# Column maxima of an attention chunk: one VectorE reduction over two PSUM banks in place of two reductions over one

## The chip, the cores and the metric

The kernel runs on one core of a Trainium2 chip. The metric is the device time of one execution in microseconds (us). The times of the kernel before are three runs; one further execution was profiled, and all rows shown come from it.

## The reference

Eight images of 64 channels and 56 x 56 pixels go through a group norm and a 3x3 convolution with a residual, then, with the 3136 pixels of an image as tokens of 64 channels, through self attention within the image, and through a mixture of 16 experts of which each token takes two. Cut to what matters here:

```python
x = x + conv3x3(group_norm(x), weight)
t = to_tokens(x)                                   # 8 x 3136 x 64
n = layer_norm(t)
q, k, v = n @ Wq.T + bq, n @ Wk.T + bk, n @ Wv.T + bv
attn = softmax(q @ k.T / 8, axis=-1)               # 3136 x 3136 per image
t = t + attn @ v
t = t + top2_of_16_experts(layer_norm(t))
```

The softmax needs, for each query, a bound on its scores to be subtracted in the exponent. The kernel computes the maximum of the query's scores over all 3136 keys.

## The kernel before

An image is cut into 7 chunks of 448 tokens (`CHUNK`), a chunk into 4 tiles of 112. There are 56 chunks over the 8 images, and the program is written out in full, with one body for each chunk and some bodies before the first and after the last. A body has 25 steps, `i` from 0 to 24, one for each block of 128 keys (`KEY_TILES`). Each engine has its own loop over the same steps, and what it does at a step stands in a fixed order, in tables (`STEPS`, `EXPERT_STEPS`, `MAXIMA`). Engines run through their own lists in order and meet by semaphores.

At a step TensorE (PE) computes the scores of the current chunk against one key block, in two matmuls (L1179 and L1181, "scores"), into one of two banks `ps_s`. ScalarE (ACT) takes their exponential (L720). At every fourth step, i = 5, 9, 13 and so on, PE weighs the values of four key blocks (L1193, eight rows of half matmuls for four instructions in the profile; "weigh"); the last group of a chunk, five key blocks, is weighed at i = 1 of the next body. In between stand the steps of the other stages: the convolution of a chunk of the next image (i = 1), token transposes (i = 3), the residual and the second norm of the chunk before (i = 4 to 10), the routing of experts and the experts themselves in pairs. An expert pair is "fx" (transpose, L1322), "hidden" (L1337), "gated" on VectorE (DVE) at i = 5, 9, 13, 17, 21 (L1039 and L1043), "turn" on PE one step later (i = 6, 10, 14, 18, 22; L1345), which waits for `hid` of DVE's L1043, and "down" (L1352).

Among this stand the maxima of the **next** chunk. A chunk needs 28 of them (`TILES`): 4 query tiles by 7 key chunks. For each, PE runs a matmul of 112 queries by 448 keys (L1156; for the last four, whose keys lie in two pieces, two matmuls of 112 and 336 columns) into one of two banks, `ps_m[m % 2]`, and DVE reduces the 448 columns to one number per query (L891, into `max_part`). Matmul m waits until the reduction of m - 2 is done, that is, until its own bank was read, while the other bank may be full or being read. How many maxima a step has says `MAXIMA`, or `MAXIMA_ROUTING` for the first chunk of an image (c = 0), in which DVE also works out the routing. In an ordinary chunk steps 0 to 3 have 1, 2, 2, 2, steps 4 to 18 one each, and steps 19 to 21 two each. Where a step has two, the first stands ahead of that step's weigh and the second behind it:

```python
if at.ahead:
    maxima(at.n + 1, at.next_u, range(done, min(done + 1, reach)))
...                                  # weigh
if at.ahead:
    maxima(at.n + 1, at.next_u, range(min(done + 1, reach), reach))
```

DVE has at each step first the reductions of that step and then its other work. After the last reduction DVE takes the maximum over the parts (L898, at i = 22), PE turns it (L1165, "shift", at i = 23), ACT writes it into row 0 of the queries (L712), and the first scores of the next chunk wait for it. For the very first chunk there is nothing to stand between: all 28 maxima are issued in one go (`maxima(0, 0, range(TILES))`).

Two other parts are named below. At i = 0 and 18 of some chunks DVE combines expert outputs that GpSimd (POOL) has gathered by indirect DMA (L1052 to L1057). POOL also scatters tokens by indirect DMA (L565) and gathers them (L586), in runs of some 2 to 20 instructions.

## Time and profile before

| | |
|---|---|
| median of 3 runs | 3720.57 us (3715.77 to 3722.61) |
| profiled execution, its own time | 3727.06 us |
| span of the profiled execution | 3725.3 us |
| granted TensorE clock, mean | 0.869 |
| busy: PE / DVE / ACT / POOL | 74% / 52% / 35% / 27% |
| chain that ended last: PE / DVE / ACT | 51% / 20% / 2% |

The profiled execution is 6.5 us over the median. Its span starts with the first instruction and ends with the last. Times in rows are microseconds from the start of the span, durations of one instruction in the groups are nanoseconds. PE's matmuls overlap: one of 448 columns is shown with 0.36 us, while the next one starts 0.20 us after it at the full clock (2.4 GHz) and 0.37 us after it at the half clock (1.2 GHz).

### The profile page before, as it was taken

How to read it: one execution, taken by the hardware profiler on the slowest of the kernel's cores; microseconds unless marked ns; L12 is line 12 of the kernel's file. 1: busy time of each engine (PE TensorE's matmuls, PEld its weight loads, DVE VectorE, ACT ScalarE, POOL GpSimd, SP SyncE). 2: the span in 40 equal slices, each digit the busy share in tenths (PEclk: the TensorE clock that was granted, in tenths of full speed). 3: DMA queues.
4: the chain of work that ended last, by engine and by line, in shares of the span. 5: the costliest groups of instructions: out<-in, count | busy, mean ns of one | idle time of the engine just before them, and what ended most of it. 6: DMA issues, size and time to landing. Idle time of an engine off the chain costs nothing.

```text
span 3725.3 us, 46578 instructions
## 1 busy us (share of the span) xinstructions
PE 2742.8 (74%) x13913; PEld 1720.2 (46%) x13913; DVE 1924.3 (52%) x5340; ACT 1320.1 (35%) x2953; POOL 1011.3 (27%) x1089
## 2 busy tenths in 40 slices
PE   0499987998688857888678857888678858882461
PEld 0255543555355534555345535555445534542350
DVE  1466664666365645666455645665456635542221
ACT  0134432444344423444334423444334423441230
POOL 4000024002412242223413242222423142216235
PEclk9689998999899979999799978999899978995665
DMA  5200001111111111111111111111111111111222
GB/s 135 57 15 16 21 26 36 34 32 42 45 36 43 39 48 48 33 42 47 46 38 47 37 49 41 41 42 44 43 32 43 28 42 38 25 41 46 54 67 45
DMA packets 222524, 156.90 MB, mean 42 GB/s; under 512 B 98512, under 2 KB 212944, under 8 KB 222288
## 3 DMA queue, kind: packets, MB, share of 16 engines
q1 hardware_dynamic: 191120, 106.94, 10.7%
q0 software_dynamic: 31168, 46.98, 5.2%
q8 instruction: 128, 2.10, 0.2%
q14 instruction: 108, 0.88, 0.1%
HBM read 89.29 MB, written 63.83 MB: 41 GB/s over the span
## 4 chain that ended last, share of the span: by engine, by line
PE 51%; DVE 20%; issue 11%; another core or an unknown queue 11%; POOL 4%; ACT 2%; DMA 0%; POOLq 0%; DVEq 0%; SPq 0%; ACTq 0%
PE ps_o L1193 12%; PE ps_m L1156 9%; DVE max_part L891 7%; PE ps_s L1179 6%; PE ps_s L1181 5%; PE ps_z L1219 4%; PE ps_x L1337 3%; PE ps_x L1352 2%; PE ps_z L1322 2%; PE ps_z L1345 2%; DVE hid L1043 1%; DVE up L1039 1%; POOL got L586 1%; POOL ln_s L604 1%
## 5 line engine op out<-in xcount | busy, mean ns | idle before, releaser
L891 DVE TENSOR_REDUCE max_part<-ps_m 112x1 f32<-112x448 f32 x1568 | 953.0, 621 | 1166.6 <-PE ps_m L1156 737.3
L720 ACT ACTIVATE prob<-ps_s 128x448 f32<-128x448 f32 x1400 | 755.4, 542 | 1123.8 <-PE ps_s L1181 852.3
L1156 PE MATMUL ps_m<-k_a,q_a 128*112 128x448 f32 (+2 forms) x1792 | 634.0, 387 | 124.5 <-DVE max_part L891 101.9
L1179 PE MATMUL ps_s<-q_a,k_a 128*128 128x448 f32 x1400 | 625.9, 447 | 49.1 <-ACT q_a L712 30.5
L1193 PE MATMUL ps_o<-prob,v_s 128*64 128x448 f32 x2800 | 648.6, 572 | 0.0
L586 POOL DMA_INDIRECT got<-sorted_y,slot x448 | 427.4, 954 | 482.7 <-DVE t_out L1057 282.6
L1181 PE MATMUL ps_s<-q_b,k_a 128*128 128x448 f32 x1400 | 531.6, 380 | 0.0
L565 POOL DMA_INDIRECT sorted_x<-xn,slot x448 | 426.8, 953 | 292.7 <-issue 246.0
L1156 PEld LDWEIGHTS ps_m<-k_a,q_a 128*112 128x112 f32 x1792 | 325.1, 188 | 328.3 <-DVE max_part L891 196.3
L604 POOL TENSOR_TENSOR ln_s<-ln_s,minus_half 112x4 f32<-112x4 f32 x56 | 58.0, 1037 | 1477.6 <-DVE ln_s L797 1477.6
L1179 PEld LDWEIGHTS ps_s<-q_a,k_a 128*128 128x128 f32 x1400 | 278.9, 199 | 253.4 <-issue 188.9
L1193 PEld LDWEIGHTS ps_o<-prob,v_s 128*64 128x64 f32 x2800 | 185.2, 141 | 299.1 <-issue 257.5
L1181 PEld LDWEIGHTS ps_s<-q_b,k_a 128*128 128x128 f32 x1400 | 280.4, 200 | 6.5 <-issue 2.7
L1345 PE MATMUL ps_z<-ident,hid 128*128 128x128 f32 x414 | 92.0, 306 | 256.2 <-DVE hid L1043 164.4
L1345 PEld LDWEIGHTS ps_z<-ident,hid 128*128 128x128 f32 x414 | 49.2, 147 | 303.8 <-DVE hid L1043 198.6
L1219 PE MATMUL ps_z<-xg,wT 128*64 128x224 f32 x1344 | 152.8, 380 | 48.0 <-ACT xg L640 48.0
L687 ACT ACTIVATE th<-ps_x 128x256 f32<-128x256 f32 x207 | 79.2, 383 | 267.1 <-PE ps_x L1337 128.4
L1337 PE MATMUL ps_x<-w_hi,fxT 128*128 x414 | 149.4, 369 | 23.4 <-issue 9.6
L1322 PE MATMUL ps_z<-ident,fx 128*128 128x128 f32 x512 | 118.5, 319 | 63.4 <-issue 37.2
L600 POOL TENSOR_TENSOR ln_s<-ln_s,minus_half 112x4 f32<-112x4 f32 x56 | 57.2, 1021 | 384.5 <-DVE ln_s L797 384.5
L1352 PE MATMUL ps_x<-w3s,hidT 128*128 x828 | 139.6, 296 | 28.5 <-issue 23.1
L683 ACT ACTIVATE fxT<-ps_z 128x256 fp32r<-128x256 f32 x256 | 98.3, 384 | 162.2 <-remote 66.2
(182 smaller groups left out, 3060.0 us busy)
## 6 DMA issues: line engine op xcount, KB each, us to landing
fx<-sorted_x SPq DMA_DIRECT2D x48, 384.0 KB
sorted_y<-fy SPq DMA_DIRECT2D x48, 320.0 KB
fx<-sorted_x SPq DMA_DIRECT2D x56, 256.0 KB
xh<-in_x SPq DMA_DIRECT2D x96, 126.0 KB
x_st<-in_x SPq DMA_DIRECT2D x100, 112.0 KB, 2.7
sorted_x<-fy POOLq DMA_DIRECT2D x24, 320.0 KB, 8.6
sorted_x<-xn,slot POOLq DMA_INDIRECT x448
got<-sorted_y,slot POOLq DMA_INDIRECT x448
```

What stands on the lines that cost most here:

```text
L565: g.indirect_dma_start(out=sorted_x[b % 2], out_offset=bass.IndirectOffsetOnAxis(ap=slot[:, b % 4, k, c * PER + j:c * PER + j + 1], axis=0 ...
L586: g.indirect_dma_start(out=got[k % 2][m][:, j, :], out_offset=None, in_=sorted_y[b % 2], in_offset=bass.IndirectOffsetOnAxis(ap=slot[:, b ...
L720: a.activation(prob[(at.n * KEY_TILES + i) % PROBS][:], ps_s[(at.n * KEY_TILES + i) % 2][:, 0:CHUNK], ACT.Exp).then_inc(s["p_ready"], 1)
L891: v.tensor_reduce(max_part[:, m % PER, m // PER:m // PER + 1], ps_m[m % 2][0:TILE, 0:CHUNK], AX.X, ALU.max).then_inc(s["max_red"], 1)
L1156: done = t.matmul(ps_m[m % 2][0:TILE, first:last], q_a[:, bass.ds(n % QUERIES, 1), j * TILE:(j + 1) * TILE].rearrange("p a c -> p (a c)"), ...
L1179: t.matmul(ps_s[t_of % 2][:, 0:CHUNK], k_a[p][:, keys], q_a[:, now, :].rearrange("p a c -> p (a c)"), start=True, stop=False)
L1181: t.matmul(ps_s[t_of % 2][:, 0:CHUNK], k_a[p][:, keys], q_b[:, now, :].rearrange("p a c -> p (a c)"), start=False, stop=True).then_inc(s[" ...
L1193: t.matmul(ps_o[side:side + CHANNELS, 0:CHUNK], v_s[u % 2][:, i, :], prob[(n * KEY_TILES + i) % PROBS][:], start=(i < 2), stop=(i >= KEY_T ...
L1219: last = t.matmul(ps_z[64 * half:64 * half + 64, 0:CHUNK // 2], wT[:, down, k, :], xg[:, top:top + ROWS // 2, k:k + SIDE], start=(down == ...
L1337: last = t.matmul((ps_x if at.attends else ps_s[f % 2])[:, j * 2 * HIDDEN:(j + 1) * 2 * HIDDEN], fxT[:, j * SLOTS:(j + 1) * SLOTS], w12[pa ...
L1345: last = t.transpose((ps_z if at.attends else ps_m[0])[:, j * SLOTS:(j + 1) * SLOTS], hid[:, j, :], ident[:])
L1352: last = t.matmul((ps_x if at.attends else ps_m[1])[:, j * CHANNELS:(j + 1) * CHANNELS], hidT[:, j * SLOTS:(j + 1) * SLOTS], w3s[:, bass.d ...
```

## The change

The two banks become one tensor of two banks. DVE reduces them in one instruction, 112 partitions by 2 by 448 elements to 112 by 2. It waits until both matmuls of a pair are done, and the matmuls of a pair wait until the reduction of the pair before is done. The maxima stand in pairs: at steps 0, 1, 2, 3, at every odd step from 5 to 19, and at 20 and 21 in an ordinary chunk; at 0, 1, 2, 3, 5, 7, 9, 10, 11, 13, 15, 17, 19 and 21 in the first chunk of an image. Both matmuls of a pair stand ahead of weigh. Lines of the changed kernel are one higher from here on (L891 becomes L892, L1156 becomes L1157).

```diff
-MAXIMA = (1, 2, 2, 2) + 15 * (1,) + (2, 2, 2)
-MAXIMA_ROUTING = (2, 2, 2, 2, 1, 2, 1, 1, 1, 2, 1, 1, 1, 2) + 7 * (1,)
+MAXIMA = (2, 2, 2, 2, 0, 2, 0, 2, 0, 2, 0, 2, 0, 2, 0, 2, 0, 2, 0, 2, 2, 2)
+MAXIMA_ROUTING = (2, 2, 2, 2, 0, 2, 0, 2, 0, 2, 2, 2, 0, 2, 0, 2, 0, 2, 0, 2, 0, 2)
...
-        ps_m = [pb(f"ps_m{i}", [128, 512]) for i in range(2)]
+        ps_m2 = pb("ps_m2", [128, 2, 512])
+        ps_m = [ps_m2[:, i, :] for i in range(2)]
...
             def reduces(n, which):
-                for m in which:
-                    dve.wait_ge(s["max_done"], ONE + n * TILES + (m + 1))
-                    v.tensor_reduce(max_part[:, m % PER, m // PER:m // PER + 1],
-                                    ps_m[m % 2][0:TILE, 0:CHUNK], AX.X, ALU.max).then_inc(s["max_red"], 1)
+                for m in which[::2]:
+                    dve.wait_ge(s["max_done"], ONE + n * TILES + (m + 2))
+                    v.tensor_reduce(max_part[:, m % PER:m % PER + 2, m // PER], ps_m2[0:TILE, :, 0:CHUNK], AX.X, ALU.max)\
+                        .then_inc(s["max_red"], 1)
...
-                    if m >= 2:
+                    if m >= 2 and m % 2 == 0:
...
-                        pe.wait_ge(s["max_red"], ONE + n * TILES + (m - 1))
+                        pe.wait_ge(s["max_red"], ONE + (n * TILES + m) // 2)
...
                     if at.ahead:
-                        maxima(at.n + 1, at.next_u, range(done, min(done + 1, reach)))
+                        maxima(at.n + 1, at.next_u, range(done, reach))
...
-                    if at.ahead:
-                        maxima(at.n + 1, at.next_u, range(min(done + 1, reach), reach))
-                        done = reach
+                    done = reach
```

The order of PE's instructions at steps 0 to 3 of an ordinary chunk, before (scores are L1179 and L1181, maxima L1156, weigh L1193, convolution L1219):

```order
L1179 MATMUL ps_s<-q_a,k_a 128x448
L1181 MATMUL ps_s<-q_b,k_a 128x448
L1156 MATMUL ps_m<-k_a,q_a 112x448
L1179 MATMUL ps_s<-q_a,k_a 128x448
L1181 MATMUL ps_s<-q_b,k_a 128x448
L1156 MATMUL ps_m<-k_a,q_a 112x448
L1193 MATMUL ps_o<-prob,v_s 64x448 x5
L1156 MATMUL ps_m<-k_a,q_a 112x448
L1219 MATMUL ps_z<-xg,wT 64x224 x12
```

and now (each line number one higher):

```order
L1180 MATMUL ps_s<-q_a,k_a 128x448
L1182 MATMUL ps_s<-q_b,k_a 128x448
L1157 MATMUL ps_m<-k_a,q_a 112x448 x2
L1180 MATMUL ps_s<-q_a,k_a 128x448
L1182 MATMUL ps_s<-q_b,k_a 128x448
L1157 MATMUL ps_m<-k_a,q_a 112x448 x2
L1194 MATMUL ps_o<-prob,v_s 64x448 x5
L1220 MATMUL ps_z<-xg,wT 64x224 x12
```

The third maximum stood behind weigh and now stands ahead of it, in a pair with the fourth, and this pair waits for the reduction of the first pair, with only two score matmuls between.

PE's order at steps 21 and 22 (turn is L1345), before:

```order
L1156 MATMUL ps_m<-k_a,q_a 112x112
L1156 MATMUL ps_m<-k_a,q_a 112x336
L1193 MATMUL ps_o<-prob,v_s 64x448 x4
L1156 MATMUL ps_m<-k_a,q_a 112x112
L1156 MATMUL ps_m<-k_a,q_a 112x336
L1179 MATMUL ps_s<-q_a,k_a 128x448
L1181 MATMUL ps_s<-q_b,k_a 128x448
L1345 MATMUL ps_z<-ident,hid 128x128 x2
```

and now:

```order
L1157 MATMUL ps_m<-k_a,q_a 112x112
L1157 MATMUL ps_m<-k_a,q_a 112x336
L1157 MATMUL ps_m<-k_a,q_a 112x112
L1157 MATMUL ps_m<-k_a,q_a 112x336
L1194 MATMUL ps_o<-prob,v_s 64x448 x4
L1180 MATMUL ps_s<-q_a,k_a 128x448
L1182 MATMUL ps_s<-q_b,k_a 128x448
L1346 MATMUL ps_z<-ident,hid 128x128 x2
```

The last maximum has moved from behind weigh to ahead of it.

DVE's order from step 5 to step 9 of an ordinary chunk (gated is L1039 and L1043, the second norm L788 to L797 and L932 to L935), before:

```order
L891 TENSOR_REDUCE max_part<-ps_m 112x1
L1039 SCALAR_TENSOR_TENSOR up<-th,ps_x 128x256
L1043 TENSOR_TENSOR hid<-up,ps_x 128x256
L891 TENSOR_REDUCE max_part<-ps_m 112x1
L788 TENSOR_REDUCE ln_s<-t_now 112x4
...
L891 TENSOR_REDUCE max_part<-ps_m 112x1
L795 TENSOR_TENSOR ln_q<-ln_c 112x256
...
L891 TENSOR_REDUCE max_part<-ps_m 112x1
L932 TENSOR_TENSOR ln_c<-ln_c,ln_s 112x256
...
L891 TENSOR_REDUCE max_part<-ps_m 112x1
```

and now:

```order
L892 TENSOR_REDUCE max_part<-ps_m 112x2
L1040 SCALAR_TENSOR_TENSOR up<-th,ps_x 128x256
L1044 TENSOR_TENSOR hid<-up,ps_x 128x256
L789 TENSOR_REDUCE ln_s<-t_now 112x4
...
L892 TENSOR_REDUCE max_part<-ps_m 112x2
L796 TENSOR_TENSOR ln_q<-ln_c 112x256
...
L933 TENSOR_TENSOR ln_c<-ln_c,ln_s 112x256
...
L892 TENSOR_REDUCE max_part<-ps_m 112x2
```

At the even steps no reduction stands ahead of DVE's other work any more; at the odd steps a joint one stands ahead of gated.

## Rows read from the trace of the kernel before

**Rows 1.** The page: busy time, share of the span and instructions of each engine.

```profile
PE 2742.8 (74%) x13913; PEld 1720.2 (46%) x13913; DVE 1924.3 (52%) x5340; ACT 1320.1 (35%) x2953; POOL 1011.3 (27%) x1089
```

**Rows 2.** The page: the chain that ended last, by engine, by line.

```profile
PE 51%; DVE 20%; issue 11%; another core or an unknown queue 11%; POOL 4%; ACT 2%; DMA 0%; POOLq 0%; DVEq 0%; SPq 0%; ACTq 0%
PE ps_o L1193 12%; PE ps_m L1156 9%; DVE max_part L891 7%; PE ps_s L1179 6%; PE ps_s L1181 5%; PE ps_z L1219 4%; PE ps_x L1337 3%; PE ps_x L1352 2%; PE ps_z L1322 2%; PE ps_z L1345 2%; DVE hid L1043 1%; DVE up L1039 1%; POOL got L586 1%; PO
```

**Rows 3.** The page's costliest groups: busy, mean ns | idle before, its releaser.

```profile
L891 DVE TENSOR_REDUCE max_part<-ps_m 112x1 f32<-112x448 f32 x1568 | 953.0, 621 | 1166.6 <-PE ps_m L1156 737.3
L1156 PE MATMUL ps_m<-k_a,q_a 128*112 128x448 f32 (+2 forms) x1792 | 634.0, 387 | 124.5 <-DVE max_part L891 101.9
```

**Rows 4.** Groups by form on DVE: other reductions, by size.

```profile
L796 DVE TENSOR_REDUCE ln_s<-ln_q 112x4 f32<-112x256 f32 x112 | 47.0, 420 | 3.8
L1008 DVE TENSOR_REDUCE slot_f<-picks 112x28 f32<-112x448 f32 x16 | 15.8, 990 | 0.6
```

**Rows 5.** Timeline, first chunk's 28 maxima: start, duration, engine, line, count [idle before].

```profile
183.44 1.16 DVE L891 TENSOR_REDUCE max_part<-ps_m 112x1 f32<-112x448 f32 x2 [0.28 <-PE ps_m L1156]
...
184.12 1.25 PE L1156 MATMUL ps_m<-k_a,q_a 128*112 128x448 f32 x2 [0.19 <-DVE max_part L891]
184.65 0.26 PEld L1156 LDWEIGHTS ps_m<-k_a,q_a 128*112 128x112 f32 x1 [0.27 <-DVE max_part L891]
184.87 1.16 DVE L891 TENSOR_REDUCE max_part<-ps_m 112x1 f32<-112x448 f32 x2 [0.28 <-PE ps_m L1156]
```

**Rows 6.** Timeline, steps 0 and 1 of an ordinary chunk.

```profile
1512.00 0.36 PE L1156 MATMUL ps_m<-k_a,q_a 128*112 128x448 f32 x1
...
1512.40 1.24 DVE L891 TENSOR_REDUCE max_part<-ps_m 112x1 f32<-112x448 f32 x2 [2.24 <-PE ps_m L1156]
...
1512.61 0.36 PE L1156 MATMUL ps_m<-k_a,q_a 128*112 128x448 f32 x1
...
1512.90 2.47 PE L1193 MATMUL ps_o<-prob,v_s 128*64 128x448 f32 x10
```

**Rows 7.** Timeline, steps 2 and 3 of the same chunk.

```profile
1518.62 0.57 PE L1156 MATMUL ps_m<-k_a,q_a 128*112 128x448 f32 x2
...
1519.03 1.16 DVE L891 TENSOR_REDUCE max_part<-ps_m 112x1 f32<-112x448 f32 x2 [2.61 <-PE ps_m L1156]
...
1519.24 0.36 PE L1181 MATMUL ps_s<-q_b,k_a 128*128 128x448 f32 x1
...
1519.71 0.99 PE L1156 MATMUL ps_m<-k_a,q_a 128*112 128x448 f32 x2
```

**Rows 8.** Timeline, steps 21 and 22 of another ordinary chunk.

```profile
1611.90 0.52 PE L1156 MATMUL ps_m<-k_a,q_a 128*112 128x112 f32 x2
...
1613.91 0.44 PE L1345 MATMUL ps_z<-ident,hid 128*128 128x128 f32 x2 [0.69 <-issue]
```

**Rows 9.** Timeline, step 6 of a first chunk of an image.

```profile
1696.25 0.44 PE L1345 MATMUL ps_z<-ident,hid 128*128 128x128 f32 x2 [0.89 <-DVE hid L1043]
```

**Rows 10.** Timeline of PE and DVE, steps 5 to 10 of a third ordinary chunk.

```profile
1635.43 0.42 DVE L1043 TENSOR_TENSOR hid<-up,ps_x 128x256 f32<-128x256 f32 x1
...
1636.71 0.38 PE L1345 MATMUL ps_z<-ident,hid 128*128 128x128 f32 x2
...
1644.98 0.44 PE L1345 MATMUL ps_z<-ident,hid 128*128 128x128 f32 x2 [1.21 <-DVE hid L1043]
```

**Rows 11.** Who waited for whom: us in total, times, longest.

```profile
DVE max_part L891 <- remote: 338.9, 51, 20.0
```

**Rows 12.** Timeline, two weighs of four key blocks, at the full and at the lower clock.

```profile
1610.24 1.72 PE L1193 MATMUL ps_o<-prob,v_s 128*64 128x448 f32 x8
...
1671.16 3.26 PE L1193 MATMUL ps_o<-prob,v_s 128*64 128x448 f32 x8
```

**Rows 13.** Stretch, its us, busy PE, PEld, DVE, ACT, POOL, granted clock, DMA share, GB/s.

```profile
182.68:200.00 17.32, 15.08 (x27) 6.68 (x27) 13.90 (x25) 0.00 (x0) 0.00 (x0) 0.50 0.01 2
```

More of the change, by code:

```diff
@@ L888, in reduces @@
             def reduces(n, which):
-                for m in which:
-                    dve.wait_ge(s["max_done"], ONE + n * TILES + (m + 1))
-                    v.tensor_reduce(max_part[:, m % PER, m // PER:m // PER + 1],
-                                    ps_m[m % 2][0:TILE, 0:CHUNK], AX.X, ALU.max).then_inc(s["max_red"], 1)
+                for m in which[::2]:
+                    dve.wait_ge(s["max_done"], ONE + n * TILES + (m + 2))
+                    v.tensor_reduce(max_part[:, m % PER:m % PER + 2, m // PER], ps_m2[0:TILE, :, 0:CHUNK], AX.X, ALU.max)\
+                        .then_inc(s["max_red"], 1)
             def max_total(n):
-                dve.wait_ge(s["max_red"], ONE + (n + 1) * TILES)
+                dve.wait_ge(s["max_red"], ONE + (n + 1) * TILES // 2)
                 dve.wait_ge(s["shiftT_done"], ONE + n)
@@ L1370, in body @@
                     for bank in (bank_turn, bank_down):
-                        bank.readers = [("max_red", ALL * TILES)]
+                        bank.readers = [("max_red", ALL * TILES // 2)]
                 bank_y.readers = [] if at.attends and at.c else \
```

## The prediction

> **What bounds the kernel now.** I read the page's first line, the chain, the costliest groups, and then the timelines of the places that the change touches. No engine is full: PE is busy for 74% of the span and DVE for 52% [rows 1]. The chain goes through PE for 51% and DVE for 20%, the maxima's matmuls and reductions among it with 9% and 7% [rows 2]. So PE's list sets the pace, with stops at which it waits for DVE; in the groups, PE waits 101.9 us for L891 itself, and DVE idles 1166.6 us ahead of it [rows 3]. DVE's busy time is thus not what is to be saved. What counts is how long PE stands at a wait, and which wait that is.
>
> **The joint instruction.** A reduction of 448 columns takes 621 ns [rows 3], one of 256 takes 420 ns [rows 4]: 1.05 ns a column, so 448 columns more cost 469 ns and the joint one takes 621 + 469 = 1.09 us. Bounds: 0.94 us (896 columns and nothing fixed) below; above, the reduction that takes 990 ns for 448 columns [rows 4], which twice is 1.98 us. I take 1.09, since the access is the contiguous one of L891 and L796, while that of L1008 is strided. Two reductions that follow each other take 1.16 us from start to end already [rows 7]: the second costs 0.54, not 0.62. So a pair saves DVE about 0.07 us, 14 pairs in 56 chunks about 55 us of an engine that is idle for half of the span. On the path I cost that at nothing.
>
> The Trainium skill, "VectorE: DVE Perf Modes", section on the TRN2 errata, gives 120 cycles plus one per element from PSUM at 0.96 GHz, which makes 0.59 us for one and 1.06 us for two banks; this trace has 0.62 for one. By its figure the sum below would be about 3 us lower.
>
> **Part 1: the first chunk's 28 maxima, on the path.** Here PE and DVE have nothing else. Before, a pair of maxima passes every 184.87 - 183.44 = 1.43 us [rows 5], at half clock [rows 13], with the matmul of one bank under the reduction of the other. Now the steps follow each other: from the reduction's end to the matmul 0.06 us, to the second matmul's start 184.65 - 184.12 = 0.53, from a matmul's start to its reduction 184.87 - 184.12 = 0.75 [rows 5], and 1.09: together 2.43. Thirteen times 1.00 more is **+13 us**.
>
> **Part 2: steps 1 and 3 of every chunk.** At full clock a reduction starts 0.40 us after its matmul starts (1512.00 to 1512.40) [rows 6]. Now the second matmul of the first pair starts at 1512.20, the joint reduction at 1512.60; it ends at 1513.69 and PE can go on at 1513.75. PE's work until then is two score matmuls, over at 1512.81. PE stands for 0.9 us, where before it went straight on to the next maximum (1512.61) and into weigh at 1512.90 [rows 6]. Behind this wait are queued weigh (2.47 us), then the convolution, and all that PE does later; nothing covers it. At step 3 the same happens with the pair of step 2: its second matmul starts at 1518.82, so the reduction ends at 1520.31, PE starts the pair at 1520.37 and its second matmul about 0.3 us later, at 1520.67. Before, the second one started at about 1519.71 + 0.99 - 0.36 = 1520.34 [rows 7]. That is 0.35 us. Together +1.25 a chunk. At step 2 weigh and the convolution cover the wait, at step 20 DVE's other work makes PE wait already now, at step 21 the "hidden" matmuls cover it, and at odd steps from 5 a pair has two steps of PE's work.
>
> The seven chunks of the first image pay all of it: **+9 us**. Of the other images I count chunks 3, 4, 5 and 7 of 7 in full, 28 chunks: **+35 us**. The second and the sixth chunk of an image have a stop soon after, for DVE and ACT at the same time, while POOL issues indirect DMAs (the "remote" idle time, 338.9 us for L891) [rows 11]; its end hangs on POOL, and I let it swallow these waits. The first chunk comes below.
>
> **Part 3: the turn.** PE's turn waits for `hid`. At step 22 the last maximum stood behind weigh, its reduction ahead of gated, and PE waited 0.69 us [rows 8]. With the maximum ahead of weigh (1.72 us) [rows 12], reduction (1.09) and gated (0.85) are nearly over when PE comes. I take -0.7 for the chunks of seven images that have a turn there and are not the first of their image, some 34: **-24 us**. At steps 6, 14 and 18 the slack in an ordinary chunk is 1636.71 - 1635.85 = 0.86 us [rows 10]; the pair's second matmul takes 0.20 of it and the longer reduction 0.47, and 0.19 are left: nothing. At step 10 PE waits already (1.21) [rows 10]. Steps 7 and 9 now have 2 x 1.09 of reductions in front of `hid` where they had three of 0.54, and the second norm starts earlier since no reduction stands at step 6; POOL's square root between, which a reduction used to fill, is open now. I take 0.2 for the same 28 chunks, **+6 us**; the ends are -0.3 and +0.6.
>
> **Part 4: the first chunk of an image.** Where it had two maxima at a step with weigh, the second one held up `hid`: 0.89 us at step 6 [rows 9], and it is built alike at 10 and 14. All three go, -2.7, against +1.25 at steps 1 and 3 and about 0.4 at step 11, where three pairs stand in a row: -1.0 for seven chunks, **-7 us**.
>
> **Part 5: the clock.** Weigh takes 1.72 us at full clock and 3.26 where the clock is lower for most of it [rows 12]. That stretch came after PE had waited. Part 2 puts 0.9 us of waiting right behind the wait for the shift. I take such a stretch in one of seven of 42 chunks, 1.6 us each: **+10 us**. The ends are 0 and +67 (all of them).
>
> Sum: 13 + 9 + 35 - 24 + 6 - 7 + 10 = +42 us. On the profiled execution's 3727 that is 3769. The runs' median is 6.5 lower, so **3762 us**. A change of 0.2%, 7.4 us, is about what a measurement of this kernel can tell from none.
>
> **Rivals.**
> *Later waits take the new ones back, and it gets faster.* Place: PE's waits at steps 4 to 18 for ACT, DVE and POOL. Only the first image and the start would then pay, 22 us, against -24 and some -14 of part 4 (its -2.7 with 0.7 of waits left): 3720.6 - 16 = 3705, and to 3698 if the shorter DVE list shows as well. It decides if less than about 0.4 of the 1.25 us reaches a chunk's end. For it: DVE is freer at even steps, and PE waits 1.21 us at step 10. Against it: the work that ends those waits is itself behind PE's step 1 in time. 0.11.
> The same page's errata section says that a fixed latency is paid per instruction and that larger tiles spread it, which speaks for this rival; the 0.07 us of the rows is all that it comes to here.
> *They cancel.* Half of part 2 and of the step 10 is swallowed: +42 - 22 - 3 - 10 (no clock), +7, 3728. 0.11.
> *The clock falls after step 1 in most chunks.* +67 instead of +10: 3819. For it, the waits at the shift and at step 1 lie together; against it, steps with as much waiting now (1.21 at step 10) mostly keep the clock. 0.11.
> The Trainium skill, "TensorE: Matmul & The Clock Gate", section on the second HAM failure mode, tells of a kernel whose clock swung because PE stood shortly between groups of matmuls as it went through PSUM banks; that is this rival.
> *The joint reduction has the strided rate.* 1.98 us: 0.9 more at steps 1 and 3, 0.7 at each of four turns, over 4 us in 50 chunks: 3950. 0.03.
> That the change does not do what it says is excluded by the order, which shows half the reductions.
>
> **Numbers.** The forecast has 0.64, its own range is 3742 to 3784 (0.2 us a chunk more or less at step 1 and 3, the ends of step 10). To hold 8 in 10 the range takes in the cancelling case, part of the faster one and part of the clock: 3718 to 3802. Slower: 0.64 + 0.11 + 0.03 = 0.78; the cancelling case lies on the edge of "same" and gives it 0.11; faster 0.11.
>
> **What the profile after would show.** The joint reduction x784 at about 1.09 us; a pair every 2.4 us in the first chunk; an idle of 0.9 us ahead of PE's pair at step 1 and of 0.5 to 1 us at step 3; no idle at step 22's turn and at step 6 of an image's first chunk; 0.2 us more at step 10; DVE's busy time some 50 us lower. The prediction is wrong if the joint reduction is not near 1.09, if a chunk of the first image is not 1.25 us longer, or if the stops with POOL move by more than 10 us in sum.

## Result and the profile after

The changed kernel takes 3838.91 us (median of four runs, 3829.49 to 3848.34), the kernel before 3718.17 on the same chip (3715.53 to 3722.61): a ratio of 1.0324 [1.0294, 1.0353], 121 us slower, where +42 was forecast and the range ended at 3802. The sign was right, the size nearly three times too small.

The page of the profile after, its busy line, its chain by line, and its two groups of the maxima:

```profile
PE 2737.6 (71%) x13913; PEld 1738.9 (45%) x13913; DVE 1856.9 (48%) x4556; ACT 1295.5 (34%) x2953; POOL 1014.4 (26%) x1089
...
DVE max_part L892 11%; PE ps_o L1194 11%; PE ps_m L1157 9%; PE ps_s L1180 6%; PE ps_s L1182 4%; PE ps_z L1220 4%; PE ps_x L1338 2%; PE ps_x L1353 2%; POOL ln_s L605 1%; PE ps_z L1323 1%; PE ps_z L1346 1%; PE ps_y L1257 1%; DVE up L1040 1%; POOL got L587 1%
...
L892 DVE TENSOR_REDUCE max_part<-ps_m 112x2 f32<-112x896 f32 x784 | 856.1, 1092 | 1276.7 <-PE ps_m L1157 784.1
L1157 PE MATMUL ps_m<-k_a,q_a 128*112 128x448 f32 (+2 forms) x1792 | 522.1, 386 | 189.9 <-DVE max_part L892 170.3
```

The joint reduction takes 1092 ns, as worked out beforehand (1.09). DVE is 67 us less busy than in [rows 1], and nobody gains by it: the reductions' share of the chain rises from 7% [rows 2] to 11%, and PE's idle time ahead of the maxima that L892 ends is 170.3 us where L891's was 101.9 [rows 3]. In the view of waits DVE's "remote" idle time ahead of the reductions, 338.9 us before [rows 11], has grown too ("remote" is idle time whose end the profile puts down to no instruction of this core):

```profile
DVE max_part L892 <- remote: 474.8, 51, 25.3
```

This row is no measure of the loss: it holds the time that DVE waited for PE to issue as well, and over the kernels below it goes another way than their times (331.6 us in the run "fence" and 250.9 in the joint reduction at the old places, both slower than the kernel before).

Where the time came from, by stretches (view of windows, whole core; columns: window, its length, busy us of PE, PEld, DVE, ACT and POOL with their instructions, granted clock, DMA share, GB/s). The windows are the time until the first scores, the first image, the other seven images up to the last chunk's start, and the rest. Before:

```profile
0.00:203.90 203.90, 63.73 (x267) 36.66 (x267) 66.56 (x188) 16.04 (x28) 45.64 (x82) 0.76 0.37 88
203.90:482.90 279.00, 259.54 (x1292) 149.18 (x1292) 183.44 (x504) 117.23 (x231) 13.65 (x14) 0.98 0.07 19
482.90:3297.00 2814.10, 2235.56 (x11476) 1393.22 (x11476) 1573.28 (x4365) 1093.77 (x2429) 768.20 (x799) 0.90 0.15 40
3297.00:3725.30 428.30, 183.98 (x878) 141.11 (x878) 101.04 (x283) 93.03 (x268) 183.78 (x194) 0.63 0.21 52
```

and after:

```profile
0.00:214.80 214.80, 61.68 (x267) 35.80 (x267) 65.69 (x174) 16.06 (x28) 45.71 (x82) 0.75 0.35 83
214.80:508.90 294.10, 260.20 (x1293) 151.41 (x1293) 175.31 (x406) 112.56 (x231) 13.66 (x14) 0.97 0.06 18
508.90:3406.70 2897.80, 2231.44 (x11477) 1411.01 (x11477) 1514.78 (x3693) 1073.80 (x2429) 770.50 (x799) 0.89 0.14 38
3406.70:3834.00 427.30, 184.24 (x878) 140.66 (x878) 101.07 (x283) 93.10 (x267) 184.54 (x194) 0.63 0.20 52
```

So +10.9 us at the start, +15.1 in the first image, +83.7 in the seven others and nothing at the end. The first two are near their terms (13 and 9). The third, where the forecast had 35 - 24 + 6 - 7 + 10 = +20, holds the error. PE has no more work there; it stands longer.

The steps themselves did what was said. At the start (timeline; start, length, instruction, idle time before it and what ended it) a pair passes every 2.28 us:

```profile
184.09 1.09 DVE L892 TENSOR_REDUCE max_part<-ps_m 112x2 f32<-112x896 f32 x1 [1.18 <-PE ps_m L1157]
185.24 1.09 PE L1157 MATMUL ps_m<-k_a,q_a 128*112 128x448 f32 x2 [1.19 <-DVE max_part L892]
186.37 1.09 DVE L892 TENSOR_REDUCE max_part<-ps_m 112x2 f32<-112x896 f32 x1 [1.18 <-PE ps_m L1157]
```

and at steps 0 to 3 of an ordinary chunk PE waits at the second pair of each two:

```profile
1564.01 0.57 PE L1157 MATMUL ps_m<-k_a,q_a 128*112 128x448 f32 x2
1564.61 1.09 DVE L892 TENSOR_REDUCE max_part<-ps_m 112x2 f32<-112x896 f32 x1 [5.15 <-PE ps_m L1157]
1565.76 0.66 PE L1157 MATMUL ps_m<-k_a,q_a 128*112 128x448 f32 x2 [0.77 <-DVE max_part L892]
...
1571.53 0.56 PE L1157 MATMUL ps_m<-k_a,q_a 128*112 128x448 f32 x2
1572.13 1.09 DVE L892 TENSOR_REDUCE max_part<-ps_m 112x2 f32<-112x896 f32 x1 [4.58 <-PE ps_m L1157]
1573.28 0.67 PE L1157 MATMUL ps_m<-k_a,q_a 128*112 128x448 f32 x2 [0.78 <-DVE max_part L892]
```

0.77 and 0.78 us of idle time, forecast as 0.9 and 0.5 to 1. The turn at step 22 and the one at step 6 of an image's first chunk follow with no wait, where there were 0.69 [rows 8] and 0.89 [rows 9]:

```profile
1615.75 0.38 PE L1346 MATMUL ps_z<-ident,hid 128*128 128x128 f32 x2
...
1749.04 0.38 PE L1346 MATMUL ps_z<-ident,hid 128*128 128x128 f32 x2
```

What is missing lies for the most part in the chunks with stops. Windows again, of a first and a second chunk of an image, after: the second takes 98 us for nearly the same matmuls, at a clock of 0.72, and POOL is busy for 46 of them:

```profile
1732.90:1789.20 56.30, 48.02 (x252) 30.42 (x252) 35.74 (x85) 24.19 (x55) 11.85 (x12) 0.97 0.14 36
1789.20:1887.40 98.20, 54.37 (x257) 34.56 (x257) 34.67 (x83) 23.94 (x56) 46.17 (x48) 0.72 0.17 47
```

The same chunks took 54.10 and 93.70 us before (same view), 2.2 and 4.5 less. The second one's beginning in the timeline after, with the pairs of steps 1, 2 and 3:

```profile
1792.53 0.66 PE L1157 MATMUL ps_m<-k_a,q_a 128*112 128x448 f32 x2 [1.82 <-DVE max_part L892]
...
1799.99 0.57 PE L1157 MATMUL ps_m<-k_a,q_a 128*112 128x448 f32 x2
...
1804.63 1.09 DVE L892 TENSOR_REDUCE max_part<-ps_m 112x2 f32<-112x896 f32 x1 [8.71 <-remote]
1805.78 1.09 PE L1157 MATMUL ps_m<-k_a,q_a 128*112 128x448 f32 x2 [4.41 <-DVE max_part L892]
...
1812.44 1.09 DVE L892 TENSOR_REDUCE max_part<-ps_m 112x2 f32<-112x896 f32 x1 [6.42 <-remote]
```

The pair of step 2 is over at 1800.56, and DVE, idle since 1795.92, starts its reduction at 1804.63, 4.07 us later. The semaphore that the two matmuls raise has its own events in the trace, and they stand at 1804.57 and 1804.61: it is the signal that is late. PE waits for DVE until 1805.78, and the pair that it then issues, over at 1806.87, is taken up at 1812.44. POOL issues an indirect DMA every 1.25 us through all of this.

How far this goes can be read for every reduction, as the time from the moment when its matmuls are over and DVE is free to its start. In the kernel before it is over 0.5 us for 89 reductions, 461 us in sum and 20.0 us at the longest; in the changed kernel for 59, 395 us in sum. The late signals as such have thus not grown. What has grown is what PE makes hang on them.

### The profile page after: what moved, and what is told of

Same layout as the page of the kernel before. It is cut to its first block, busy times and chain, and to the rows that moved or that the text cites. A ratio compares the mean times of both kernels' runs of the same rounds, so it can differ in the third digit from the quotient of the medians.

```text
span 3834.0 us, 45734 instructions
## 1 busy us (share of the span) xinstructions
PE 2737.6 (71%) x13913; PEld 1738.9 (45%) x13913; DVE 1856.9 (48%) x4556; ACT 1295.5 (34%) x2953; POOL 1014.4 (26%) x1089
## 4 chain that ended last, share of the span: by engine, by line
PE 45%; DVE 22%; another core or an unknown queue 15%; issue 9%; POOL 4%; ACT 3%; DMA 0%; POOLq 0%; DVEq 0%; ACTq 0%; SPq 0%
DVE max_part L892 11%; PE ps_o L1194 11%; PE ps_m L1157 9%; PE ps_s L1180 6%; PE ps_s L1182 4%; PE ps_z L1220 4%; PE ps_x L1338 2%; PE ps_x L1353 2%; POOL ln_s L605 1%; PE ps_z L1323 1%; PE ps_z L1346 1%; PE ps_y L1257 1%; DVE up L1040 1%; POOL got L587 1%
## 5 line engine op out<-in xcount | busy, mean ns | idle before, releaser
L892 DVE TENSOR_REDUCE max_part<-ps_m 112x2 f32<-112x896 f32 x784 | 856.1, 1092 | 1276.7 <-PE ps_m L1157 784.1
L1194 PE MATMUL ps_o<-prob,v_s 128*64 128x448 f32 x2800 | 662.1, 582 | 0.0
L1157 PE MATMUL ps_m<-k_a,q_a 128*112 128x448 f32 (+2 forms) x1792 | 522.1, 386 | 189.9 <-DVE max_part L892 170.3
L1157 PEld LDWEIGHTS ps_m<-k_a,q_a 128*112 128x112 f32 x1792 | 309.2, 192 | 318.7 <-DVE max_part L892 270.3
L1220 PE MATMUL ps_z<-xg,wT 128*64 128x224 f32 x1344 | 182.3, 385 | 48.0 <-ACT xg L641 48.0
L1220 PEld LDWEIGHTS ps_z<-xg,wT 128*64 128x64 f32 x1344 | 121.9, 148 | 97.1 <-ACT xg L641 50.2
```

Source lines behind the costliest of these rows:

```text
L892: v.tensor_reduce(max_part[:, m % PER:m % PER + 2, m // PER], ps_m2[0:TILE, :, 0:CHUNK], AX.X, ALU.max)\
L1157: done = t.matmul(ps_m[m % 2][0:TILE, first:last], q_a[:, bass.ds(n % QUERIES, 1), j * TILE:(j + 1) * TILE].rearrange("p a c -> p (a c)"), ...
L1194: t.matmul(ps_o[side:side + CHANNELS, 0:CHUNK], v_s[u % 2][:, i, :], prob[(n * KEY_TILES + i) % PROBS][:], start=(i < 2), stop=(i >= KEY_T ...
L1220: last = t.matmul(ps_z[64 * half:64 * half + 64, 0:CHUNK // 2], wT[:, down, k, :], xg[:, top:top + ROWS // 2, k:k + SIDE], start=(down == ...
```

## Experiments

Three theories stood at the outset: (A) that the new wait of a pair for the reduction of both banks (the "fence") costs nearly all of it, as the prediction had it; (B) that the order (tables and places) costs a good part by itself, since matmuls at even steps filled waits of PE; (C) that POOL's bursts of indirect DMAs delay every handshake, of which the change has more one behind the other. The edits are against the kernel before unless it says otherwise. As it turned out, the runs came from chips of two kinds, between which the same kernel before differs by 15%: about 3720 us (3695 on one), and about 3150 us. I call them chips **with stops** and **without stops**. No chip was used on a second occasion, as far as the runs tell, so that the chip and the occasion are not told apart. Each ratio is against the kernel before on the same chip.

**Order alone**: the new tables, both maxima of a step ahead of weigh, but single reductions, each bank with its own wait.

```diff
-MAXIMA = (1, 2, 2, 2) + 15 * (1,) + (2, 2, 2)
-MAXIMA_ROUTING = (2, 2, 2, 2, 1, 2, 1, 1, 1, 2, 1, 1, 1, 2) + 7 * (1,)
+MAXIMA = (2, 2, 2, 2, 0, 2, 0, 2, 0, 2, 0, 2, 0, 2, 0, 2, 0, 2, 0, 2, 2, 2)
+MAXIMA_ROUTING = (2, 2, 2, 2, 0, 2, 0, 2, 0, 2, 2, 2, 0, 2, 0, 2, 0, 2, 0, 2, 0, 2)
...
-                        maxima(at.n + 1, at.next_u, range(done, min(done + 1, reach)))
+                        maxima(at.n + 1, at.next_u, range(done, reach))
...
-                    if at.ahead:
-                        maxima(at.n + 1, at.next_u, range(min(done + 1, reach), reach))
-                        done = reach
+                    done = reach
```

> Kernel before with the tables of the change and both maxima of a step ahead of weigh, but a reduction and a wait for each bank, as before. Theory A (the fence: PE's pair waits for a reduction of both banks, and nothing is under it): this kernel is near the one before, 3700 to 3735 us, with steps 21 and 22 shorter. Theory B (the order: the matmuls that stood at even steps filled waits of PE, and pairs leave those open): 60 us or more of the 120 are here, 3780 or more. Theory C (a burst of GpSimd's indirect DMAs delays every handshake, and the change has more of them one behind the other): near before, as A.

3769.3 us, 1.0139 [1.0121, 1.0158]: +49 us without any joint instruction, between what A and B had.

**Fence**: the same, and the first matmul of a pair waits for both single reductions of the pair before, as the change has it, still with two reductions.

```diff
-                    if m >= 2:
+                    if m >= 2 and m % 2 == 0:
-                        pe.wait_ge(s["max_red"], ONE + n * TILES + (m - 1))
+                        pe.wait_ge(s["max_red"], ONE + n * TILES + m)
```

> As the last, but the first matmul of a pair waits for the reductions of both banks of the pair before, while the reductions stay two. What it adds to the last is the fence without the joint instruction. Theory A: 80 to 110 us over the last, near the changed kernel (3839), since two reductions take 1.16 us where the joint one takes 1.09, and the first starts one matmul earlier. Theory B: 20 us or less over the last.

3799.41 us, 1.0222 [1.0205, 1.0239]: 30 us more. The rest to the changed kernel's 121 is the one instruction itself, some 41 us. So no single part costs nearly all: order, fence and instruction cost about 49, 30 and 41.

**Joint reduction at the old places**: the changed kernel with the old tables and split, DVE reducing a pair at the step of its second matmul.

```diff
-                for m in which[::2]:
+                for m in [m - 1 for m in which if m % 2]:
```

> The joint reduction and the fence of the change, with the tables of before and the maxima at their old places (one matmul a step from 4 to 18, the second of a step behind weigh). Theory A: the fence costs here too, and more at the one-a-step stretch, where a pair's first matmul waits for a reduction that could only start one step before: 3820 to 3900. Theory B: the even steps have their matmul again, so most of the loss goes: below 3780.

4027.06 us, 1.0832 [1.0814, 1.085], more than was expected. With one matmul a step the wait falls right behind every second reduction, in the middle of the steps; PE's idle time before the maxima is ended by L892 for 477.3 us:

```profile
L1157 PE MATMUL ps_m<-k_a,q_a 128*112 128x448 f32 (+2 forms) x1792 | 679.6, 414 | 519.6 <-DVE max_part L892 477.3 <-issue 37.6 <-ACT hidT L693 1.1
```

So given fence and joint instruction, the new order is worth some 190 us, while single reductions with a wait each are the faster ones in the old order. Which of the two, fence or instruction, needs the pairing was not run.

**Both ahead of weigh**: the kernel before with that edit alone (the first diff without its tables).

> Kernel before with one edit: where a step has two maxima, both stand ahead of weigh. Tables and single reductions as before. All theories: the turn at step 22 no longer waits (0.7 us a chunk), while PE may stand at step 1 for the first bank: 3690 to 3715, if the gain of step 22 reaches the end.

3705.01 us, 0.9964 [0.9951, 0.9976]. A gain of 15 us, as expected before the run, where parts 3 and 4 of the prediction have 24 + 7 x 2.7 = 43 from it. And the tables then cost 64 us on top. Both were odd, and the stops were the suspect.

**Plain DMAs**: POOL's 896 indirect DMAs, scatters and gathers, become plain ones of the same size with fixed rows. This leaves out the sorting of tokens by expert: the experts work on other tokens, and the output is not that of the reference. The edit, in which the gathers change alike:

```diff
-                    g.indirect_dma_start(
-                        out=sorted_x[b % 2], out_offset=bass.IndirectOffsetOnAxis(ap=slot[:, b % 4, k, c * PER + j:c * PER + j + 1], axis=0),
-                        in_=xn2[:, c * PER + j, :, :].bitcast(f32).rearrange("p a c -> p (a c)"), in_offset=None).then_inc(s[f"scattered{m % 2}"], 16)
+                    row = (k * TILES + c * PER + j) * TILE
+                    g.dma_start(sorted_x[b % 2][row:row + TILE, :],
+                                xn2[:, c * PER + j, :, :].bitcast(f32).rearrange("p a c -> p (a c)"))\
+                        .then_inc(s[f"scattered{m % 2}"], 16)
...
```

In the kernel before:

> Kernel before with GpSimd's 896 indirect DMAs replaced by plain ones of the same size to and from fixed rows (tokens are not sorted by expert, so the experts work on other tokens). All theories: the long stops of VectorE and ScalarE that end on an unknown releaser go, the second chunk of an image (88.7 us on average) falls towards the 53 of the others; 3300 to 3550 us. If they do not go, it was not the indirect DMAs.

In the changed kernel:

> The changed kernel with the same replacement. Theory C (bursts delay every handshake, and the change adds handshakes one behind the other): most of what order and fence do not account for goes, the difference to the last run falls from 119 us to 70 or less. Theories A and B (fence and order in undisturbed steps): the difference stays 95 to 125 us.

3047.79 (0.9671 [0.9651, 0.9692]) and 3125.01 (0.9917 [0.9892, 0.9942]): the change costs 77 us here, between what the theories had. But this chip ran the kernel before itself in 3150.3 us, with its indirect DMAs: the chip has no stops to take away. The same pair again on another such chip:

> Kernel before with GpSimd's indirect DMAs replaced by plain ones to and from fixed rows (tokens are not sorted by expert). If this chip has the stops (kernel before near 3720 us): 3048 again would show that the stops come with the indirect DMAs; 3400 or more would show that they come with anything that GpSimd issues. On a chip without them: 3048 again, no news.

> The changed kernel with the same replacement. With stops on this chip and theory C (70 of the 120 us are stops met at another place): 75 us over the last run, as on the chip without stops. If the change itself costs 120 whenever the chip is of this kind, then 110 or more over the last.

3051.45 (0.9676 [0.9657, 0.9695]) and 3125.78 (0.9915 [0.9898, 0.9932]), 74 us. To see whether the stops come with the indirect DMAs, the first of them had to run on a chip that has stops:

> Kernel before with plain DMAs (tokens are not sorted by expert), for a chip with stops: 3050 if they come with the indirect DMAs, 3400 or more if with any DMA that GpSimd issues. On a chip without: 3050 again.

3049.62 against 3694.83, 0.8256 [0.8242, 0.827], and DVE's waits have no "remote" row any more (view of DVE's waits; L892 is here the single reduction):

```profile
DVE max_part L892 <- PE ps_m L1157: 657.6, 537, 3.9
```

With plain DMAs both kinds of chip take the same 3050 us; with indirect ones they are 3150 and 3700. The stops are thus a matter of the indirect DMAs on some chips, and cost this kernel some 550 us there. (Before the first of these runs 3300 to 3550 us had been expected with plain DMAs.)

**The ladder on a chip without stops.** Changed kernel, order alone, both ahead of weigh, and on another such chip the fence:

> The changed kernel once more, beside the kernel before on this chip. The last set of runs had the kernel before at 3150 us where the first chip had it at 3720, without the stops under GpSimd's indirect DMAs. If this chip has them (before near 3720): 3839 again, +3.2%. If it does not (before near 3150): theories A and B expect what the pair with plain DMAs showed, +2.5% or 75 to 80 us; a theory by which the stops make the loss expects +1% or less.

> Order alone again, on the chip of this set. Chip with stops: +49 us again. Without: the order cost is in undisturbed steps by theory B, so +25 to +45 us; by a theory in which the order only meets the stops at other places, within 10 us of before.

> Both maxima ahead of weigh again. Chip with stops: -15 us again. Without: step 22 gives 0.7 to 1.1 us in about 41 chunks and steps 6, 10 and 14 of the first chunks 0.9 each: -35 to -50 us.

> The new order and the fence with two reductions. With stops: 3799 again. Without: order alone had 3142, the changed kernel 3207; theory A puts the fence at 0.13 to 0.3 us less than the joint one per wait, so 3165 to 3185, the fence +25 to +40 and the joint instruction the rest.

Each rung against the one above it, in us, from the medians (before, then the edits one on top of the other):

| | with stops | without stops |
|---|---|---|
| both ahead of weigh | -15, 0.9964 [0.9951, 0.9976] | -44, 0.9867 [0.9849, 0.9886] |
| new tables as well (order alone) | +64, 1.0139 [1.0121, 1.0158] | +29, 0.9953 [0.9932, 0.9974] |
| fence as well | +30, 1.0222 [1.0205, 1.0239] | +35, 1.0068 [1.0051, 1.0085] |
| one instruction (the change) | +41, 1.0324 [1.0294, 1.0353] | +31, 1.0165 [1.0146, 1.0184] |
| in all | +121 | +50 |

Each ratio is against the kernel before on the rung's own chip; a rung's microseconds are its median's distance from the kernel before, less that of the rung above. By these intervals a rung is uncertain by some 6 to 12 us. Fence and instruction together cost 71 us with stops and 66 without, nearly the same. The order costs 49 with stops and gives 15 without, where +25 to +45 had been expected: 64 of the 70 us between the two totals. The total of +50 lies between what the theories had for such a chip, 75 to 80 us and at most 1% (32 us).

The waits of the changed kernel without stops show fence and instruction alone, with no "remote" row:

```profile
L892 DVE TENSOR_REDUCE max_part<-ps_m 112x2 f32<-112x896 f32 x784 | 855.9, 1092 | 759.3 <-PE ps_m L1157 755.0
L1157 PE MATMUL ps_m<-k_a,q_a 128*112 128x448 f32 (+2 forms) x1792 | 493.5, 367 | 154.0 <-DVE max_part L892 151.4
```

against 41.2 us that L891 ends with both ahead of weigh and nothing else:

```profile
L1156 PE MATMUL ps_m<-k_a,q_a 128*112 128x448 f32 (+2 forms) x1792 | 595.2, 369 | 58.4 <-DVE max_part L891 41.2
```

The fifth chunk of an image in three parts, steps 0 and 1, 2 and 3, 4 to 21 (windows, chip without stops), ahead of weigh:

```profile
1669.20:1675.80 6.60, 6.48 (x41) 3.86 (x41) 1.80 (x3) 2.04 (x4) 0.00 (x0) 1.00 0.01 2
1675.80:1679.20 3.40, 2.98 (x13) 1.75 (x12) 2.48 (x5) 1.81 (x5) 0.00 (x0) 1.00 0.01 2
1679.20:1712.90 33.70, 32.06 (x182) 21.32 (x182) 26.13 (x77) 17.18 (x40) 11.75 (x12) 1.00 0.17 43
```

and the changed kernel:

```profile
1733.80:1741.30 7.50, 6.73 (x43) 3.99 (x43) 2.19 (x2) 2.07 (x4) 0.00 (x0) 1.00 0.01 2
1741.30:1744.90 3.60, 2.63 (x14) 1.84 (x13) 2.03 (x3) 1.79 (x5) 0.00 (x0) 1.00 0.00 0
1744.90:1779.80 34.90, 32.24 (x180) 20.94 (x180) 24.79 (x66) 16.86 (x41) 11.78 (x12) 1.00 0.16 42
```

At full clock in every part, steps 0 to 3 take 11.1 us in place of 10.0, near part 2's 1.25. Steps 4 to 21 take 34.9 in place of 33.7, and there the sum has +0.2 alone. But the order alone has a part of both already (its steps 2 and 3 take 3.40):

```profile
1684.20:1691.40 7.20, 7.02 (x43) 4.10 (x43) 2.32 (x4) 2.06 (x4) 0.00 (x0) 1.00 0.01 2
1694.80:1729.10 34.30, 32.00 (x181) 21.20 (x181) 25.17 (x75) 16.77 (x40) 11.74 (x12) 1.00 0.17 43
```

By the starts of the scores in this chunk, over the four kernels of the ladder, steps 0 and 1 take 6.65, 7.19, 7.38 and 7.52 us, and steps 4 to 21 take 33.65, 34.28, 34.55 and 34.99. So 0.54 us of what part 2 puts down to the wait for both banks comes with the order, which moves one more maximum to step 0 and both of step 1 ahead of weigh; and at steps 4 to 21 the tables have 0.63, the fence 0.27 and the instruction 0.44.

**Places.** For the tables' part of that 1.2 us I looked at step 8, whose maximum they took away. With it (ahead of weigh), the step runs from its first scores at 1685.94 to the next step's:

```profile
1686.23 0.37 PE L1181 MATMUL ps_s<-q_b,k_a 128*128 128x448 f32 x1
1686.44 0.37 PE L1156 MATMUL ps_m<-k_a,q_a 128*112 128x448 f32 x1
1686.91 0.39 PE L1337 MATMUL ps_x<-w_hi,fxT 128*128 x1
1687.68 0.36 PE L1179 MATMUL ps_s<-q_a,k_a 128*128 128x448 f32 x1
```

1.74 us; and without (order alone), from 1701.47:

```profile
1701.76 0.36 PE L1181 MATMUL ps_s<-q_b,k_a 128*128 128x448 f32 x1
1702.41 0.38 PE L1337 MATMUL ps_x<-w_hi,fxT 128*128 x1 [0.30 <-issue]
1703.18 0.37 PE L1179 MATMUL ps_s<-q_a,k_a 128*128 128x448 f32 x1
```

1.71 us. The maximum lay in a wait of PE and cost nothing; at the odd step it costs its 0.20 us. The tables move eight maxima away from the even steps 4 to 18. Over the fifth chunks, each odd step that gets one is 0.20 us longer; the even steps 8, 10, 12 and 16 are no shorter for the loss (by 0.1 at the most), while 4, 6, 14 and 18 are 0.2 shorter. So four of the eight lay in waits, and the tables cost some 0.6 us a chunk there, not 1.6. Two kernels put the pairs at 0, 2, 4, 6, 8, 9, 10, 12, 13, 14, 16, 17, 18 and 20 of every chunk, joint and single:

> The joint reduction and fence, with the pairs at steps 0, 2, 4, 6, 8, 9, 10, 12, 13, 14, 16, 17, 18, 20 in all chunks: even steps, where PE waits for something else, and no two pairs with less than a long piece of PE's work between. Theory B: both the waits at 1, 3, 20, 21 and the open even steps go, about 60 of the 120 us come back: 3740 to 3785. Theory A without B (the loss is the fence wherever it stands): above 3800.

> The same places with a reduction and a wait for each bank. Theory B: even steps hold two matmuls that fill PE's waits, so it is at least 40 us below the order-alone run (3769), near the run with both ahead of weigh (3705): 3690 to 3730. If the order does not matter as such, it stays near 3769.

These expectations are for a chip with stops, and the runs came from one without.

3184.14 (1.0104 [1.0081, 1.0127]) and 3120.47 (0.9904 [0.9883, 0.9925]): better than their counterparts with the change's tables (1.0165 and 0.9953), so places do count, but single reductions beat the joint one there too, by 64 us.

**The best order** keeps single reductions and both ahead of weigh, leaves the first image's tables, and gives the other images two maxima at each even step up to 18, one at each odd step from 5 to 17 and one at step 20:

```diff
+MAXIMA_LATER = (2, 0, 2, 0, 2, 1, 2, 1, 2, 1, 2, 1, 2, 1, 2, 1, 2, 1, 2, 0, 1)
...
-    return sum((MAXIMA if at.c else MAXIMA_ROUTING)[:i + 1])
+    return sum((MAXIMA_LATER if at.u else MAXIMA if at.c else MAXIMA_ROUTING)[:i + 1])
```

> Single reductions, both maxima ahead of weigh; the first image keeps the old tables (its even steps have no waits to fill), the others have 2 maxima at every even step to 18, one at the odd steps 5 to 17 and one at 20. By theory B this is the fastest: on a chip without stops 3085 to 3110 where before has 3150, on one with them 3670 to 3700 where it has 3720. If filling steps is not what counts, it is no better than the run before it.

> Single reductions, both ahead of weigh, filling places. With stops: 3670 to 3700 where before has 3720; if the stops are met at worse places, above 3705 as with both ahead of weigh alone. Without: -2.0% again.

> The best version once more, for a chip with stops (kernel before near 3720): 3670 to 3700 there; above 3705 if its order meets the stops at worse places, as the order of the change does. On a chip without: -1.8% again.

3094.7 us (0.9804 [0.9785, 0.9822]) and 3097.67 (0.9829 [0.9812, 0.9845]) without stops, 3647.22 (0.9871 [0.9855, 0.9888]) with stops, there 23 us below the expected range: it beats both kernels on both kinds of chip. It is one order among many and was found on the one kind; nothing says it is the best.

## Why the prediction was right in sign and wrong in size

- **The joint instruction** (1.09 us, nothing gained on the path from a freer DVE): right, 1092 ns. The freer DVE showed nowhere.
- **Part 1** (+13): +10.9. The pair takes 2.28 us, not 2.43. The prediction's 0.53 us from one matmul to the next is read off a weight load that itself waited for a reduction ([rows 5], `0.27 <-DVE max_part L891`); without that wait the second matmul starts 0.38 us after the first. Fence and instruction share it, by the kernels between: the time until the first scores is 206.2 us with the order alone, 211.8 with the fence and 214.8 after.
- **Part 2, the first image** (+9, seven chunks in full): +15.1 us. Order alone has 280.7 us there and the fence 284.1, so 10 of the 15 come with the instruction. The mean granted clock there is 0.97, with the fence 0.99: some of it is a lower clock in single chunks, for which part 5 had its +10. Estimate from the mean clocks of the two traces, 0.983 before and 0.968 after: some 9 us more of the image are at the half clock, worth at most 5 us. In the seven other images the matmuls that meet the half clock go from 900 to 1004; at 0.17 us each, the most that one of 448 columns loses, that is at most 18 us.
- **Part 3, the turn and part 4** (-24 and -19 of part 4's sum): 44 measured for 43 without stops. With stops only 15 is left.
- **The rest of the sum** (13 + 9 + 35 + 6 + 10 and part 4's 12, thus +85): without stops 29, 35 and 31, 94 before rounding. On these chips the +42 forecast met +50. Part of that is luck: the forecast left the second and sixth chunks out for their stops, which these chips do not have (14 chunks at 1.25 + 0.2 would be 20 us more), its 35 us of part 2 belong for about a half to the order, and the costs of tables, fence and instruction at steps 4 to 21 were hardly in it.
- **The failed step** is in part 2: "its end hangs on POOL, and I let it swallow these waits". The chunk lengths show it (from a chunk's first scores to the next chunk's, mean of images 2 to 8, one trace each, us; the last row has the prediction's terms of parts 2, 3 and 4; the fourth chunk has no turn at step 22):

| chunk of its image | 1 | 2 | 3 | 4 | 5 | 6 | 7 |
|---|---|---|---|---|---|---|---|
| before | 52.7 | 88.7 | 62.4 | 44.5 | 52.8 | 53.5 | 55.4 |
| after | 53.6 | 91.9 | 63.7 | 48.1 | 53.9 | 55.1 | 55.5 |
| difference | +0.9 | +3.2 | +1.3 | +3.6 | +1.2 | +1.6 | +0.2 |
| forecast | -1.0 | -0.7 | +0.75 | +1.45 | +0.75 | -0.7 | +0.75 |

  The second and sixth chunks, whose waits the stops were to swallow, cost 34 us over the seven images, where the sum had -10. In the second chunk step 1 is 2.5 us longer and step 3 is 5.0 us longer, several times the 0.9 and 0.35 of part 2, and the stops after them give only some of it back (steps 4, 6 and 19 are 1.3, 3.0 and 1.9 us shorter). The fourth chunk costs 26 us where the sum had 10, the first 6 where it had -7.

  The same "swallowing" was applied to the costs of two chunks and to no gain. On the chips with stops the gains fall to a third (15 of 44), and the tables' cost more than doubles (64 of 29). The first is what an end that hangs on POOL does: PE comes to the stop earlier and waits longer. In the first chunk of an image, the turns of steps 6, 10 and 14 wait 0, 0.26 and 0 us in place of 0.89, 1.02 and 0.90, and then the turn of step 18 waits in a stop:

```profile
1774.42 1.09 DVE L892 TENSOR_REDUCE max_part<-ps_m 112x2 f32<-112x896 f32 x1 [5.83 <-remote]
1776.84 0.69 PE L1346 MATMUL ps_z<-ident,hid 128*128 128x128 f32 x2 [4.05 <-DVE hid L1044]
```

  In the trace before, that turn had waited 0.23 us and stood 43.6 us from the chunk's start (1722.71 - 1679.10), now 43.9 (1776.84 - 1732.90): nothing is left of the gain. As for the second, by the traces of order alone and ahead of weigh on both kinds of chip, 32 of the 35 us by which the tables cost more with stops lie in the seven later images: 18 in the second chunks (+2.4 us with stops, -0.2 without) and 9 in the sixth (+1.7 against +0.5). In the second chunk they lie again at steps 1 and 3. The fourth chunk, which I had counted as undisturbed, shows the other side. There the tables cost little more with stops than without (2.1 and 1.6 us), but fence and instruction cost 2.2 against 0.4, since they make PE depend on a reduction that sits behind a late handshake. The matmuls of a pair are over at 1552.7, DVE is free at 1553.15 and takes them up at 1554.24, while POOL issues gathers, and PE's next pair waits 2.30 us:

```profile
1550.79 0.94 POOL L587 DMA_INDIRECT got<-sorted_y,slot  x1 [0.30 <-issue]
1552.03 0.93 POOL L587 DMA_INDIRECT got<-sorted_y,slot  x1 [0.30 <-issue]
1552.11 0.57 PE L1157 MATMUL ps_m<-k_a,q_a 128*112 128x448 f32 x2
1554.24 1.09 DVE L892 TENSOR_REDUCE max_part<-ps_m 112x2 f32<-112x896 f32 x1 [1.08 <-remote]
1555.39 0.77 PE L1157 MATMUL ps_m<-k_a,q_a 128*112 128x112 f32 x4 [2.30 <-DVE max_part L892]
```

- **Terms that the sum lacked**: half of the matmuls of even steps lay in PE's waits and were free (step 8 above), at odd steps they are not. Part 3 had weighed what the pairs add at odd steps, and only against `hid`. Fence and instruction at steps 4 to 21, 0.7 us in a fifth chunk, stood in the sum with 0.2.
- **Step 10** (0.2 us more): right in size; over the fifth chunks of images 2 to 8 the wait goes from 0.70 to 0.90 us in the mean. [rows 10], with 1.21, is a seventh chunk; there it is 1.40 now. In the fourth chunk of an image 1.18 became 1.65:

```profile
1539.80 0.44 PE L1346 MATMUL ps_z<-ident,hid 128*128 128x128 f32 x2 [1.65 <-DVE hid L1044]
```

- **The rivals**: later waits did not take the new ones back, nor did they cancel. The clock did not fall after step 1 in most chunks: its mean is 0.863 in place of 0.869, the fifth chunk above, without stops, runs at 1.00, and the count of matmuls at the half clock given above leaves it at most 18 us in the seven images, where this rival has 67. The reduction has not the strided rate. Of what the prediction named as making it wrong, two came true: a chunk of the first image is more than 1.25 us longer (15.1 / 7 = 2.2), and the "remote" time moved by 136 us, not by under 10, though that row is no measure of the loss, as said.

**What stays open.** With plain DMAs the change costs 74 to 77 us, with indirect ones on chips without stops 50, in the same chunks and instructions; these 25 us are not explained. The changed kernel's first and seven other images take 294.1 and 2350.2 us with indirect DMAs without stops and 294.1 and 2342.1 with plain ones, nearly the same, so that the 25 us are rather something that the kernel before loses to the indirect DMAs and the changed one does not; but the kernel before was not traced on a chip without stops. How the tables' cost meets single stops within a chunk was not taken apart. Nor was it tried to spread POOL's indirect DMAs out, though the stops, with some 550 us, are worth far more than anything here.

## What to carry to other kernels

Two banks that one instruction reads are one buffer: the writer must wait for the reader, and the saving per instruction (0.07 us of an engine with idle time, 784 times) was paid for with some 66 us on the engine that sets the pace. Read off how much of an engine's list lies in its own waits before work is moved: a matmul in a wait is free and moved elsewhere is not; what did pay was to let a maximum go ahead of the weighing matmuls, so that its reduction is over when the turn needs DVE. And a gain ahead of a stop whose end hangs on another queue is to be counted at nothing, a new round trip between engines within it at several us (steps 1 and 3 of the second chunk: 2.5 and 5.0), of which the stop's end gives back only a part.

## What the runs showed of the hardware that I had not expected

The same kernel takes 3720 (or 3695) us on some chips and 3150 on others. On the slow kind a semaphore that PE has raised reaches DVE late while POOL issues indirect DMAs, one each 1.25 us: by up to 20.0 us in the kernel before, and the more of these DMAs lie in the last 10 us, the later (mean lag 0.02 us with none to two of them, 1.9 with six, 6.0 with eight). ACT has "remote" waits in the same traces (`prob`, 212.1 us in 44 pieces, before). In the four traces of the ladder without stops, with as many indirect DMAs, no reduction starts more than 0.5 us late and there is no "remote" row. Plain DMAs of the same size bring both kinds to 3050 us. By traces alone I had read "remote" as a wait that belongs to the kernel; it is one that comes with the kind of DMA, on some chips (or occasions) only. Why they differ no run here shows.
